# Attention block: row maxima of a head pair by 64-row matmuls in the two halves of the array

## What is computed

```
x_n = _group_norm(x, gn_w, gn_b)
q, k, v = _conv1x1(x_n, wq, bq), _conv1x1(x_n, wk, bk), _conv1x1(x_n, wv, bv)
q, k, v = (to_heads(q), to_heads(k), to_heads(v))
attn = jnp.einsum('bhqd,bhkd->bhqk', q, k) * hd ** (-0.5)
attn = jax.nn.softmax(attn, axis=-1)
out = jnp.einsum('bhqk,bhkd->bhqd', attn, v)
return x + _conv1x1(out.transpose(0, 1, 3, 2).reshape(bsz, c, h, wd), wp, bp)
```

## Time and profile before

| | |
|---|---|
| time, median of 3 runs | 374.97 us (374.83 to 375.06) |
| span of the profiled execution | 373.5 us |
| time of the profiled execution itself | not given beside its span; the median of the runs is 1.5 us above the span |
| TensorE, matmuls busy | 358.6 us (96%) |
| VectorE busy | 309.5 us (83%) |
| ScalarE busy | 311.7 us (83%) |
| POOL busy | 257.9 us (69%) |
| maxima on TensorE (L583) | 240 matmuls of 128 rows, 16 more of 64 rows (L691) |
| reductions on VectorE (L884) | 256, 687 ns each |
| granted TensorE clock | 1.000 |

### The profile page before, as it was taken

How to read it: one execution, slowest core, us unless ns; L and a number is a source line. 1 busy time by engine, 2 the same in 40 slices (tenths; PEclk the granted TensorE clock), 3 DMA queues, 4 the chain that set the end, 5 groups by cost and what they waited for, 6 DMA issues and landing times.

```text
span 373.5 us, 11249 instructions
## 1 busy us (share of the span) xinstructions
PE 358.6 (96%) x4581; PEld 227.6 (61%) x4581; DVE 309.5 (83%) x569; ACT 311.7 (83%) x393; POOL 257.9 (69%) x227
## 2 busy tenths in 40 slices
PE   1999999999999999999999999999999999999996
PEld 1734575656566665756666566656657666665674
DVE  4799888889978788889988788888888888899784
ACT  1758799989778999988887999988878888889883
POOL 5045887778496887949667796958758495757722
PEclk9999999999999999999999999999999999999999
DMA  6045250252532530342633430022542432050113
GB/s 215 17 129 148 44 123 9 30 156 57 110 116 63 116 100 2 83 132 46 136 121 73 93 92 30 17 72 44 126 146 45 89 84 73 2 182 19 31 32 112
DMA packets 38731, 30.92 MB, mean 83 GB/s; under 512 B 23820, under 2 KB 31512, under 8 KB 38680
## 3 DMA queue, kind: packets, MB, share of 16 engines
q1 hardware_dynamic: 37936, 29.15, 31.4%
q10 hardware_dynamic: 744, 1.06, 0.8%
HBM read 9.44 MB, written 4.19 MB: 37 GB/s over the span
## 4 chain that ended last, share of the span: by engine, by line
PE 76%; SPq 9%; DVE 4%; ACT 4%; DMA 3%; issue 2%; DVEq 1%; ACTq 0%
PE gen L524 16%; PE st L604 12%; PE st L605 12%; PE mx L583 11%; PE pv L627 7%; PE pv L630 7%; PE pv L629 7%; DMA q_max<-shift 3%; SPq L415 2%; SPq L394 2%; DVE mx L884 2%; PE st L524 1%; ACT st L808 1%; ACT p_hi L801 1%; DVE p_lo L905 1%
## 5 line engine op out<-in xcount | busy, mean ns | idle before, releaser
L884 DVE TENSOR_REDUCE mx<-mx 128x1 f32<-128x512 f32 x256 | 173.4, 687 | 31.5 <-PE mx L583 25.5
L801 ACT ACTIVATE p_hi<-st 128x1024 f16<-128x1024 f32 x127 | 130.3, 1026 | 39.2 <-PE st L605 38.2
L1128 POOL TENSOR_TENSOR p_lo<-p,p_hi 128x1024 f16<-128x1024 f32 x62 | 132.1, 2132 | 32.6 <-ACT p L808 32.5
L627 PE MATMUL pv<-v_hi,p_hi 128*128 128x65 f16 x1024 | 105.7, 194 | 0.5 <-DVE o L913 0.5
L630 PE MATMUL pv<-v_hi,p_lo 128*128 128x65 f16 x1024 | 105.9, 194 | 0.0
L629 PE MATMUL pv<-v_lo,p_hi 128*128 128x64 f16 x1024 | 105.7, 193 | 0.0
L627 PEld LDWEIGHTS pv<-v_hi,p_hi 128*128 128x128 f16 x1024 | 94.5, 98 | 12.9 <-DVE o L913 2.5
L629 PEld LDWEIGHTS pv<-v_lo,p_hi 128*128 128x128 f16 x1024 | 93.6, 98 | 14.1
L604 PE MATMUL st<-q_twice,k_both 128*128 128x512 f16 x256 | 97.2, 380 | 1.6 <-DMA q_max<-shift 0.9
L605 PE MATMUL st<-q_max,k_one 65*128 65x512 f16 x256 | 97.3, 380 | 0.0
L630 PEld LDWEIGHTS pv<-v_hi,p_lo 128*128 128x128 f16 x1024 | 93.7, 97 | 0.0
(11 more groups left out here) (173 smaller groups left out, 466.5 us busy)
## 6 DMA issues: line engine op xcount, KB each, us to landing
q_twice<-st_hi_q SPq DMA_DIRECT2D x64, 64.0 KB, 2.1
xres<-in_x_dram SPq DMA_DIRECT2D x4, 1024.0 KB, 5.4
out_dram<-y SPq DMA_DIRECT2D x13, 256.0 KB, 2.8
xin<-in_x_dram SPq DMA_DIRECT2D x6, 512.0 KB, 4.4
k_both<-st_hi_k SPq DMA_DIRECT2D x16, 128.0 KB, 2.3
k_one<-st_hi_k SPq DMA_DIRECT2D x16, 128.0 KB, 2.4
q_max<-st_lo_q SPq DMA_DIRECT2D x32, 64.0 KB, 2.1
k_both<-st_lo_k SPq DMA_DIRECT2D x16, 128.0 KB, 2.3
```

Of the source, the lines that this page charges most:

```text
L627: nc.tensor.matmul(pv_v[:, q, :], hi, vh, start=k == 0 and q == 0, stop=False, skip_group_check=True)
L801: nc.scalar.activation(p_hi[:, G % PR, :, :], scores, ACT.Exp, scale=SM_SCALE / M_SCALE)
L884: nc.vector.reduce_max(mx8[:, U % 2, tile, part:part + 1], mxb[j % 2][:, :], AX.X)\
L1128: nc.gpsimd.tensor_tensor(p_lo[:, G % PR, :, :], p_full(G), p_hi[:, G % PR, :, :], ALU.subtract)\
```

## The change

Units 0 to 3 of the first image keep their maxima. From the second head pair of the first image on, the two units of a head pair with the same query half are handled together, as V = U // 2: for each of eight parts (four query tiles, two key halves) two matmuls of 64 rows, one head in rows 0 to 63 and the other in rows 64 to 127, each into a bank of its own, and one reduction over both banks. They use the high parts alone. The first query half reads `kq_hi` itself, the second `q_twice` and `k_both`; for that, `k_both` of the second head of a pair now holds the high part in rows 64 to 127. Two pairs stand together in each even slot, from ten slots ahead on: one in `st[1]`, the empty scores banks of the odd slots, one in the two mx banks, which are one tensor now. Head pair 1 of the first image has its eight pairs in slots 8 to 13 by a table, in the mx banks alone. Join, shift and copy are done for both heads at once, every eight slots; the copy is two DMAs. POOL overwrites `kq_hi` only when the maxima that read it are through.

```diff
+    SINGLES = 4
+    PAIR_AHEAD = 10
+    FIRST_PAIRS = {8: (0,), 9: (1,), 10: (2, 3), 11: (4,), 12: (5, 6), 13: (7,)}
...
-        mxb = [pb("mx0"), pb("mx1")]
+        mx = pb("mx", 2)
+        mxb = [mx[:, 0:512], mx[:, 512:1024]]
...
+        def single_maxima(G):
+            U, n = divmod(G + MX_AHEAD, SPU)
+            return [("one", U, 2 * n), ("one", U, 2 * n + 1)] if U < SINGLES else []
+        def pair_maxima(G):
+            V, m = divmod(G + PAIR_AHEAD, 2 * SPU)
+            if G in FIRST_PAIRS:
+                return [("two", SINGLES // 2, m) for m in FIRST_PAIRS[G]]
+            if m % 2 or not SINGLES // 2 < V < B * UNITS // 2:
+                return []
+            return [("two", V, m), ("two", V, m + 1)]
...
+        def in_scores_bank(V, m):
+            return V > SINGLES // 2 and m % 2 == 0
+        def reduced_at(G):
+            first = [item for item in maxima_at(G) if item[0] == "one" or item[1] == SINGLES // 2
+                     or in_scores_bank(*item[1:])]
+            later = [item for item in pair_maxima(G - 1) if item[1] > SINGLES // 2 and not in_scores_bank(*item[1:])]
+            return first + later
...
@@ shift_to_row, on SP
-                wait(sp, s_shift, U + 1)
-                sp.dma_start(q_max[D:D + 1, head, halves(half)], shift[:, U % 2, :]).then_inc(s_shift_dma, 16)
+                wait(sp, s_shift, joined(U))
+                for h in units_joined(U):
+                    sp.dma_start(q_max[D:D + 1, head - U % 2 + h, halves(half)], shift[:, U // 2 % 2, h, :])\
+                      .then_inc(s_shift_dma, 16)
...
@@ on TensorE
+            def pair_of_maxima(V, m):
+                b, head, half = unit(2 * V)
+                tile, part = pair_part(m)
+                if half == 0:
+                    wait_hi(pe, "q", nth(head // 2, 0, b) + 1)
+                    wait_hi(pe, "k", nth(head // 2, part, b) + 1)
+                elif m == 0:
+                    wait(pe, s_dup_k, 16 * 6 * (V // 2 + 1))
+                    wait(pe, s_dup_q[1], 16 * 6 * (V // 2 + 1))
+                if in_scores_bank(V, m):
+                    wait(pe, s_exp, 2 * SPU * V - PAIR_AHEAD + m)
+                    bank = st[1]
+                else:
+                    wait(pe, s_mx_free, place_of["two", V, m] - (V > SINGLES // 2))
+                    bank = mx
+                for h in range(2):
+                    rows = slice(h * D, (h + 1) * D)
+                    if half == 0:
+                        queries, keys = kq_hi["q"][rows, tile_of(0, tile)], kq_hi["k"][rows, halves(part)]
+                    else:
+                        queries = q_twice[rows, head + h, tile_of(1, tile)]
+                        keys = k_both[rows, head + h, halves(part)]
+                    last = nc.tensor.matmul(bank[:, h * HALF:(h + 1) * HALF], queries, keys, start=True, stop=True)
+                last.then_inc(s_mx_full, 1)
...
@@ scores
+                if pair_in_bank(G) is not None:
+                    wait(pe, s_mx_free, pair_in_bank(G) + 1)
...
@@ row_max, on VectorE
+                    tile, part = pair_part(j)
+                    bank = st[1] if in_scores_bank(n, j) else mx
+                    nc.vector.reduce_max(mx8[:, n % 2, :, tile, part],
+                                         bank[:, :].rearrange("p (h k) -> p h k", h=2), AX.X).then_inc(s_mx_free, 1)
...
@@ slot, on VectorE
-                if top:
-                    row_max(U, n)
+                for item in tops[:1]:
+                    row_max(*item)
...
@@ high, on POOL
+                elif (i, b) > (0, 0):
+                    gone = 2 * (2 * b + i - 1)
+                    if kind == "k":
+                        wait(pool, s_mx_full, place_of["two", gone, (j + 1) * QT - 1] + 1)
+                    elif j == 0:
+                        wait(pool, s_mx_full, all_full("two", gone))
```

More of the change, by code:

```diff
@@ new lines, in maxima_at, with pair_in_bank @@
+        def maxima_at(G):
+            return single_maxima(G) + pair_maxima(G)
+        before_slots = [("one", U, j) for U in range(2) for j in range(MXJ if U == 0 else QT)]
+        in_order = before_slots + [item for G in range(TOTAL) for item in maxima_at(G)]
+        place_of = {item: n for n, item in enumerate(in_order)}
+        def in_scores_bank(V, m):
+            return V > SINGLES // 2 and m % 2 == 0
+        def pair_in_bank(G):
+            here = [item for item in pair_maxima(G - 1) if in_scores_bank(*item[1:])]
+            return place_of[here[0]] if here else None
@@ L286, in tile_of, with joined, units_joined, rows_in @@
+        def joined(U):
+            return U + 1 if U < SINGLES else SINGLES + (U - SINGLES) // 2 + 1
+        def units_joined(U):
+            return range(U % 2, U % 2 + 1) if U < SINGLES else range(2)
+        def rows_in(U):
+            return U + 1 if U < SINGLES else 2 * (U // 2) + 2
+        def complete_at(G):
+            done = [item for item in reduced_at(G) if place_of[item] + 1 == all_full(*item[:2])]
+            return [(2 * n if kind == "two" else n) for kind, n, _ in done]
         def tile_of(half, tile):
@@ L419, in slot @@
                 b, g = place(G)
-                U = shift_at(G)
-                if U is not None:
+                for U in complete_at(G - 1):
                     shift_to_row(U)
@@ L463, in first_high_keys @@
                 wait_hi(sp, "k", 2)
-                sp.dma_start(k_both[0:D, h, :], kq_hi["k"][rows, :]).then_inc(s_first[h], 16)
+                sp.dma_start(k_both[rows, h, :], kq_hi["k"][rows, :]).then_inc(s_first[h], 16)
                 sp.dma_start(k_one[0:D, h, :], kq_hi["k"][rows, :]).then_inc(s_first[h], 16)
@@ L580, in maximum @@
                 _, head, half = unit(U)
-                wait(pe, s_mx_free, MXJ * U + j - 1)
+                if j == 0 and U == 2:
+                    pe.wait_ge(s_first_top, 16 * 2)
+                elif j == 0:
+                    wait(pe, s_dup_k, 16 * 6)
+                    wait(pe, s_dup_q[1], 16 * 6)
+                n = place_of["one", U, j]
+                wait(pe, s_mx_free, n - (in_order[n - 1][0] == "one"))
                 tile, part = mx_part(U, j)
-                nc.tensor.matmul(mxb[j % 2][:, :], q_twice[:, head, tile_of(half, tile)], k_both[:, head, halves(part)],
+                nc.tensor.matmul(mxb[j % 2], q_twice[:, head, tile_of(half, tile)], k_both[:, head, halves(part)],
                                  start=True, stop=True).then_inc(s_mx_full, 1)
+            def pair_of_maxima(V, m):
[14 more added lines that the diff above has]
+                for h in range(2):
+                    rows = slice(h * D, (h + 1) * D)
+                    if half == 0:
[5 more added lines that the diff above has]
+                last.then_inc(s_mx_full, 1)
+            def maximum(item):
+                (single_maximum if item[0] == "one" else pair_of_maxima)(*item[1:])
             def scores(G):
@@ L690, in first_maximum @@
                 wait(pe, s_mx_free, MXJ * U + j - 1)
-                nc.tensor.matmul(mxb[j % 2][:, :], kq_hi["q"][rows, tile_of(0, j % QT)], kq_hi["k"][rows, half],
+                nc.tensor.matmul(mxb[j % 2], kq_hi["q"][rows, tile_of(0, j % QT)], kq_hi["k"][rows, half],
                                  start=True, stop=True).then_inc(s_mx_full, 1)
```

103 lines of the change are left out of this document (55 added, 48 removed).

## The result

The changed kernel takes 378.68 us (median of 4 runs, 378.12 to 379.70), beside 375.01 for the kernel before on the same chip: a ratio of 1.0101, 95% interval 1.0083 to 1.0118. It is slower by 1%, where 373.2 us and a gain had been forecast. The profiled execution's span is 377.0 us, 3.5 more than before.

What follows compares the result with a forecast made beforehand. TensorE was taken to bound most stretches, ScalarE or VectorE some. Terms -8.0 + 3.3 + 2.4 + .5 = -1.8 gave a span of 371.7, with 1.5 carried over 373.2 us; range 366 to 382.

Steps and rivals of the forecast that it cites:

- The sign: Whole kernel: a gain was forecast, 373.2 us; chances faster .54, same .12, slower .34.
- TensorE's part: Even slots 14 to 116: four 128-row matmuls become two 64-row pairs, .21 us gained in 38 groups, -8.0 us.
- The excursion: TensorE's switch to 64 rows and back with two pairs: .65 us in place of .87, .22 of it beyond the matmuls.
- no overlap: Rival: a pair's two matmuls on TensorE do not overlap, excursion 1.08, about 391 us; chance .07.
- VectorE late in every group: Rival: slower reductions and a later VectorE delay the odd scores in all 38 groups, about 379 us; chance .17.
- The wait behind v_lo: Slots 26 to 106: v_lo delays the reduction, odd scores start at 3.20 not 2.90; .30 lost 11 times, +3.3 us.
- Slots 8 and 9: TensorE's pair waits for the single ahead in the shared mx banks to be reduced: 1.2 us a slot, +2.4.
- Slots 10 to 13: Waits for the mx banks fall into time without projections: 0 us.
- The end: Slots 112 onwards: rounds of 4.83 against 4.37 cost 1.0 us, fewer shift waits give back .5: +.5.
- the boundaries: Slots 116, 120, 124: only one of three still waits for a shift, -.5 us.
- The rest, at nothing: Shift rows, VectorE's reductions, POOL's waits and early inputs: 0 us; second shift row .8 late three times, half of 4.0 saved.
- The middle: Slots 18 to 109: forecast at -4.7 us.

Runs made afterwards that it cites:

- run 4: Changed kernel with both matmuls of a pair reading the same 64-row half (second head's maxima left out, shifts lowered): 396.29 us, ratio 1.0566 to the kernel before.
- Run 1: Changed kernel with half of head pair 1's maxima left out (four pairs in slots 10 to 13, shift lowered): 375.26 us, ratio 1.0012.
- run 2: Changed kernel with three of head pair 1's eight pairs (slots 8, 10, 12) put into the odd slots' empty scores banks: 377.05 us, ratio 1.0060.
- run 5: Changed kernel with head pair 1's eight pairs spread over slots 4 to 13, five of them in the scores banks: 376.61 us, ratio 1.0026.
- run 7: Changed kernel with a semaphore for each shift row, so the first head's scores wait for the first row alone: 375.45 us, ratio .9996.
- run 6: Changed kernel with the last head pair's eight pairs one to a slot, slots 110 to 117, all in the mx banks: 376.81 us, ratio 1.0040.
- run 11: run 9 with ScalarE's four normalisations of the next image in slots 2, 4, 6 and 7 instead of 0, 2, 4 and 6: 369.15 us, ratio .9847.
- run 3: Changed kernel with the last head pair's eight pairs one to a slot, slots 109 to 116, all in the mx banks: 378.38 us, ratio 1.0102.
- run 9: Changed kernel with the changes of run 5, run 6 and run 7 together: 370.98 us, ratio .9891.
- run 10: run 9 with head pair 1's pairs starting from slot 6, none in slot 4, four in the scores banks: 369.81 us, ratio .9871.
- run 12: run 9 with the changes of run 10 and run 11 together: 368.99 us, ratio .9844.

## Why the prediction was wrong

The sign was wrong, the time inside the range. Its steps, in its order:

- **TensorE's part: right.** The excursion was put at .65 us with full overlap and is .65; without overlap at 1.08 and is 1.08 (run 4). Two plain slots were to take 5.15 and take 5.15. That rival, no overlap, is out; so is the one with VectorE late in every group.
- **The wait behind v_lo: right.** In slot 96 the even scores start at 288.87, the odd ones at 292.11, 3.24 behind (forecast 3.20). What it costs can be read where no other wait stands beside it: slots 40 to 44, 72 to 76 and 104 to 108, a group with a v job and the group that forms its v_lo, gain .10 or .11 on the kernel before, where two plain groups gain .40, so .3 is lost each time, as forecast (the second group alone takes 5.60, not the 5.45 named, and the first 5.08). The timeline of VectorE in slot 96:

```profile
290.14 0.69 DVE L1004 SCALAR_TENSOR_TENSOR v_lo<-gen,v_hi 128x512 f16<-128x512 f32 x1
290.74 1.22 DVE L990 TENSOR_REDUCE mx<-st 128x2 f32<-128x1024 f32 x1
```

  The reduction of 1,024 takes 1.22, as on the line of the earlier trace rows.
- **Slots 8 and 9: right in kind, .4 short** (2.77 for 2.4).
- **Slots 10 to 13: this step failed.** "Such waits fall into time that has no projections", it said, and gave nothing; they cost 2.20 us, and .36 follows in slots 14 to 17. Two things were overlooked. A pair in the shared banks cannot start before the pair ahead of it is reduced, so each of the six waits (2.5 us in all) stands in TensorE's queue ahead of the next scores. And VectorE's reductions take longer: in slots 8 to 13 eight pairs of 1.22 and four singles of .69, 12.5 us, stand where twelve singles took 8.2, so that VectorE is busy 17.14 us there (13.42 before) in slots that took 15.37. Run 1 shows that the head pair costs it all; run 2 takes away 2.1 us of waits for the banks and leaves 2.9, with one bank wait of .9 still in it; of these 2.9 run 5 gets back 1.1 by spreading the pairs, two more of them in the scores banks. That VectorE's crowding is what remains is argued, not shown.
- **The end: mis-sized.** The round of 4.83 was right (4.89 and 4.88 in slots 114 to 118), but it was set against 4.37, the mean of slots 113 to 117; slots 112 to 118 took 4.07, 4.26 and 4.48 before and take 4.61, 4.89 and 4.88, so the three rounds cost 1.57, not 1.0. And the boundaries were to give .5 back: slots 110 to 112 and 118 to 122 cost .40 instead (+.29, +.68 and -.57), for the two rows' joint wait stands there too; run 7 takes .86 off the end. +1.97 in place of +.5; run 6 gives 1.8 of it back.
- **"The rest, at nothing": the shift rows were even in the middle, not at the end.** The forecast saw the second row .8 late at one boundary of an image, three times, and set that against half of the old 4.0 us. Waits for the joint count stand at slots 24, 48, 56, 80, 112 and 120. By run 7 they are worth 2.5 us in slots 18 to 110 and .9 behind them (3.9 by ratio in all); gone in return are these 2.2 us of the kernel before in slots 18 to 110:

```profile
PEld st L604 <- DMA q_max<-shift: 2.2, 4, 0.8
```

- **The middle: its agreement is partly luck.** One loss there was in no term: ScalarE's wait for z_b at slots 32 and 64, which run 11 removes. Slots 32 to 34 and 64 to 66 take 6.37 us each, 5.94 before. In run 7 the middle is 249.98 - 243.14 = 6.84 better than before. Without the old shift waits (2.2) and with the z_b wait added back (.9) that leaves some 5.5 for the groups alone, where 4.7 had been forecast: the groups gained .8 more than the sum said, and the z_b wait took as much away. The split is an estimate from these waits; no run parts the terms one by one.

The differences, stage by stage, make up the 5.3 us between the forecast's -1.8 and the +3.5 of the span: slots 10 to 17 2.6, the end 1.5, slots 8 and 9 .4, the middle .4, the start .5. What stays open is why the second row's landing varies between 2.0 and 3.3 us: the transpositions of the output stand behind it on SP at every boundary, and nine of the 14 second rows land after 2.0 us all the same.

## What to carry to other kernels

A scheme that needs its input earlier has to be caught up with once, where it starts: count what the busiest engine gets to do there, and spread it, before the gain of the steady part is summed. When two things are joined into one step, ask of every wait behind it whether it now waits for the later of the two. When a sum comes out right in one stage, look whether two of its errors cancelled. And an order that costs a little may guard a bank that another engine wants: moving v_lo to save .3 us a group cost .8.

## What was not expected of the hardware

A second 64-row matmul in the other half of the rows starts within .01 us of the first and costs nothing else, but going to 64 rows and back costs .22 us each time (.09 on entering, .03 on the first pair's step, .10 on leaving): two pairs share one such price, a pair alone pays it whole. The Trainium skill, "TensorEngine Tiling (Array Packing)", "Key Properties", says that a change of tiling mode drains TensorE; the trace agrees, and puts .22 us on it.

A wait on TensorE can cost more than its length. In the profiles of runs 3, 4 and 5 the granted clock falls once among the slots from its upper level to .50 (1.2 GHz) for 3.4 us, and each time TensorE had just stood still for 1.8 us: for a reduction in slot 109 (run 3), for the shift rows ahead of slot 120 (runs 4 and 5). The changed kernel's profile has a wait of 1.8 us ahead of slot 120 too, and keeps 1.00. So such a wait doesn't always bring the fall; what decides it, and whether the wait is the cause, no run shows. The kernel before and runs 6 and 9 to 12, with no wait of TensorE over 1.6 us among the slots of their profiles, have no execution with a mean clock under .999; but run 7, with none over 1.2, has two of ten at .994 and .995.
